# A tokeniser whose gate weights are loaded once for TensorE, and an attention start with a PSUM bank for each piece

## The chip, the cores and the metric

The kernel runs on one core of one Trainium2 chip. The metric is the device time of one execution in microseconds (us). The kernel before took 2230.97 us (median of three runs, 2230.33 to 2231.43). All numbers are fp32 in memory.

## What is computed

Eight images of 256x256 are passed through a three-level Haar wavelet, gated, and rebuilt; the rows of each image and 77 text rows form 333 tokens of width 256. Four pairs of attention and feed-forward layers follow. The change touches the first two parts only:

```python
a1, det1 = haar(x);  a2, det2 = haar(a1);  a3, det3 = haar(a2)   # det: 3 bands each
gate_a   = sigmoid(flat(a3) @ Wa + ba)                            # 1 number per image
gate_l   = softmax(flat(det_l) @ Wd_l + bd_l)                     # 3 numbers per image and level
h        = inverse_haar(gate_a * a3, gate_l * det_l)              # 8 x 256 x 256
h        = concatenate([h, txt], axis=1)                          # 8 x 333 x 256
h        = h + attention16(layernorm(h))                          # 16 heads of 16
```

The dots of the gates run over 12288 numbers for each of the three outputs at the finest level.

## The kernel before

**Tiling.** `tokenise` (L118) puts 16 image rows of one image on one partition, so 16 partitions hold an image and 128 hold all eight. VectorE does the analysis (L240 to L258). The gate weights of each of ten outputs are replicated in SBUF: each image's 16 partitions get their own copy, by 40 DMAs (L161), and VectorE multiplies and sums them with ten `tensor_tensor_reduce` (L270, L277). One small matmul with a matrix of ones per image (L232) sums over 16 partitions; VectorE and ScalarE form sigmoid and softmax (L282 to L307). VectorE then does the synthesis (L320 to L328), level 1 in two halves. SyncE writes each half of the image to a scratch tensor in DRAM (L165, 16 DMAs, one for each half and batch element) and reads it back with 111 tokens on the partitions (L169 for token tiles 0 and 1 of an element; ScalarE issues the 34 image rows of tile 2 at L224). VectorE computes mean and variance per element (L107 to L112), GpSimd a Newton-like refinement of the inverse root in seven operations (L194 to L206). A block ends with a barrier of all engines, and `attention16` is the next block.

**First attention.** Batch elements are pipelined. For an element, `norm` makes `xn`, TensorE transposes it (pieces "x"), makes q and k (pieces "qk", four of them), v (pieces "v"), then scores. All pieces share one PSUM bank `psM`: piece n+1 waits until piece n has been copied out (`piece_out`). q and k are split in a high and a low part; SyncE writes both to DRAM (L482, L483) and reads them back in stacks (L492, eight DMAs of 16 partitions for each of the four pieces). `scores` wait for the stacks (`stack_in`). For batch element 0 the pieces stand in `START`, ahead of the loop; TensorE's first piece waits for all constants (`consts` 3), among them memsets of GpSimd. Then `scores` runs nine steps ahead of the exponentials, and VectorE's `largest` (L567) takes the maxima of each score tile; for the other elements the pieces are put between steps by the table `AT`.

What orders the work here is the program order on each engine and the two hardware DMA queues, one of SyncE and one of ScalarE.

Of the kernel before, what the change touches and what calls it, by code (L numbers as in the profile page):

```python
# [24 lines left out]
B = 8  # L25
# [9 lines left out]
E = 8  # L35

# [14 lines left out]
class Shared:  # L51
# [15 lines left out]
    def early(self, ctx):  # L67

        sb = lambda name, shape: ctx.enter_context(self.nc.sbuf_tensor(name, shape, F32))
        self.cols = sb("cols", [128, len(CNAMES), KT])  # L70
        self.rows = sb("rows", [TT, len(RNAMES), D])
        self.w_last = sb("w_last", [128, 3, KT, D])
        self.weights_in = ctx.enter_context(self.nc.semaphore("weights_in"))
        self.late_weights_in = ctx.enter_context(self.nc.semaphore("late_weights_in"))
# [43 lines left out]
def tokenise(nc, sh, ins, h0):  # L118
    RB = 16
    n1, n2, n3 = 8 * 128, 4 * 64, 2 * 32  # L120
    with ExitStack() as ctx:
        sb = lambda name, shape, dt=F32: ctx.enter_context(nc.sbuf_tensor(name, shape, dt))
        sem = lambda name: ctx.enter_context(nc.semaphore(name))
# [6 lines left out]
        a3 = sb("a3", [128, 2, 32])  # L130
        det = [sb("det1", [128, 3, n1]), sb("det2", [128, 3, n2]), sb("det3", [128, 3, n3])]
        wd = [sb("wd1", [128, 3, 3 * n1]), sb("wd2", [128, 3, 3 * n2]), sb("wd3", [128, 3, 3 * n3])]
        wa = sb("wa", [128, n3])
        gb = sb("gb", [128, 10])
        gs = sb("gs", [128, 10])
        group = sb("group", [128, 128])
        dots = sb("dots", [128, 10])
# [3 lines left out]
        ps = ctx.enter_context(nc.psum_tensor("ps_gate", [128, 512], F32))  # L141
        var2 = sb("var2", [TT, NT])
        wa_in, txt_in, h_done = (sem(n) for n in ("wa_in", "txt_in", "h_done"))
        img_in = [sem(f"img_in{i}") for i in range(2)]
        h0_out, h_in = ([sem(f"{n}{b}") for b in range(B)] for n in ("h0_out", "h_in"))
        wd_in = [[sem(f"wd_in{lv}{j}") for j in range(3 if lv == 0 else 1)] for lv in range(3)]
        dots_done, summed, z_ready, exp_done, image_ready, group_ready = (
            sem(n) for n in ("dots_done", "summed", "z_ready", "exp_done", "image_ready", "group_ready"))
        const_ready = sem("const_ready")
        block = ctx.enter_context(nc.Block())  # L150

        @block.sync
        def _(sync):
            rows = ins["x"].rearrange("(p r) c -> p r c", r=RB)
            for half in range(2):
                sync.dma_start(img[:, 8 * half:8 * half + 8, :], rows[:, 8 * half:8 * half + 8, :]).then_inc(img_in[half], 16)
            for lv in (2, 1, 0):
                for j, arrived in enumerate(wd_in[lv]):
                    part = slice(j, j + 1) if lv == 0 else slice(0, 3)
                    for b in range(B):  # L160
                        sync.dma_start(wd[lv][16 * b:16 * b + 16, part, :], ins[f"wd{lv}"][:, part, :]).then_inc(arrived, 16)  # L161
            for half in range(2):
                sync.wait_ge(image_ready, half + 1)
                for b in range(B):
                    sync.dma_start(h0[b, 0:IMG, :].rearrange("(p r) c -> p r c", r=RB)[:, 8 * half:8 * half + 8, :],  # L165
                                   out[16 * b:16 * b + 16, 8 * half:8 * half + 8, :]).then_inc(h0_out[b], 16)
            for b in range(B):
                sync.wait_ge(h0_out[b], 32)
                sync.dma_start(sh.h[:, NT * b:NT * b + 2, :],  # L169
                               h0[b, 0:2 * TT, :].rearrange("(t p) c -> p t c", p=TT)).then_inc(h_in[b], 16)  # L170
            sync.wait_ge(sh.weights_in, 48)

        @block.gpsimd
        def _(pool):
            nc.gpsimd.memset(sh.ident[:, :], 0.0)
            nc.gpsimd.memset(group[:, :], 1.0)
            nc.gpsimd.memset(sh.eps[:, :], EPS)
            nc.gpsimd.memset(sh.mhalf[:, :], -0.5)
            pool.drain()
            nc.gpsimd.affine_select(out=sh.ident[:, :], in_=sh.ident[:, :], compare_op=ALU.not_equal, fill=1.0,  # L180
                                    base=0, pattern=[[-1, 128]], channel_multiplier=1)
            g3 = group[:, :].rearrange("p (g r) -> p g r", r=16)
            nc.gpsimd.affine_select(out=g3, in_=g3, compare_op=ALU.is_ge, fill=0.0,
                                    base=0, pattern=[[-16, 8], [0, 16]], channel_multiplier=1)
            pool.drain()
            nc.gpsimd.affine_select(out=g3, in_=g3, compare_op=ALU.is_ge, fill=0.0,
                                    base=15, pattern=[[16, 8], [0, 16]],
                                    channel_multiplier=-1).then_inc(group_ready, 1)
            g = nc.gpsimd
            eps, mh = sh.eps[0:TT, 0:NT], sh.mhalf[0:TT, 0:NT]  # L190
            for b in range(B):
                pool.wait_ge(h_done, b + 1)
                var, r = sh.mv[:, NT * b:NT * b + NT, 1], sh.rs[:, NT * b:NT * b + NT]
                g.tensor_tensor(var2[:, :], var, eps, ALU.add)  # L194
                pool.drain()
                g.tensor_tensor(r, var2[:, :], mh, ALU.pow)
                pool.drain()
                g.tensor_tensor(var2[:, :], r, r, ALU.mult)
                pool.drain()
                g.tensor_tensor(var2[:, :], var2[:, :], var, ALU.mult)  # L200
                pool.drain()
                g.tensor_tensor(var2[:, :], var2[:, :], eps, ALU.add)
                pool.drain()
                g.tensor_tensor(var2[:, :], var2[:, :], mh, ALU.pow)
                pool.drain()
                g.tensor_tensor(r, r, var2[:, :], ALU.mult)  # L206
                pool.drain()

        @block.scalar
        def _(act):  # L210
            act.dma_start(wa[:, :], ins["wa"]).then_inc(wa_in, 16)
            act.dma_start(gb[:, :], ins["gb"].partition_broadcast(128)).then_inc(wa_in, 16)
            act.dma_start(sh.cols[:, :, :], ins["cols"]).then_inc(sh.weights_in, 16)
            act.dma_start(sh.h[IMG - 2 * TT:TT, 2:NTILES:NT, :], ins["txt"].rearrange("b q c -> q b c")).then_inc(txt_in, 16)
            for arrived in wd_in[0]:
                act.wait_ge(arrived, 16 * B)
            act.dma_start(sh.w[:, 0:3, :, :], ins["w"][:, 0:3, :, :]).then_inc(sh.weights_in, 16)
            act.dma_start(sh.rows[:, :, :], ins["rows"].partition_broadcast(TT)).then_inc(sh.weights_in, 16)
            act.wait_ge(z_ready, 1)
            nc.scalar.activation(ez[:, 0:1], z[:, 0:1], ACT.Exp, scale=-1.0)  # L220
            nc.scalar.activation(ez[:, 1:10], z[:, 1:10], ACT.Exp).then_inc(exp_done, 1)
            for b in range(B):
                act.wait_ge(h0_out[b], 32)
                act.dma_start(sh.h[0:IMG - 2 * TT, NT * b + 2, :], h0[b, 2 * TT:IMG, :]).then_inc(h_in[b], 16)  # L224
            act.dma_start(sh.w[:, 3:, :, :], ins["w"][:, 3:NW, :, :]).then_inc(sh.late_weights_in, 16)
            act.dma_start(sh.w_last[:, :, :, :], ins["w"][:, NW:, :, :]).then_inc(sh.late_weights_in, 16)

        @block.tensor
        def _(pe):
            pe.wait_ge(group_ready, 1)  # L230
            pe.wait_ge(dots_done, 1)
            nc.tensor.matmul(ps[:, 0:10], group[:, :], dots[:, :], start=True, stop=True).then_inc(summed, 1)  # L232

        @block.vector
        def _(dve):
# [7 lines left out]
            def analysis(src, rows, cols, approx, details):  # L243
# [3 lines left out]
                if src is img:  # L247
                    for half in range(2):
                        dve.wait_ge(img_in[half], 16)
                        columns(img, 8 * half, 8 * half + 8, cols)  # L250
                else:
                    columns(src, 0, rows, cols)
                dve.drain()
                dt = details[:, :, :].rearrange("p j (r c) -> p j r c", c=cols // 2)
                v.tensor_tensor(approx, s_[:, 0:rows:2, :], s_[:, 1:rows:2, :], ALU.add)
                v.tensor_tensor(dt[:, 0], s_[:, 0:rows:2, :], s_[:, 1:rows:2, :], ALU.subtract)
                v.tensor_tensor(dt[:, 1], d_[:, 0:rows:2, :], d_[:, 1:rows:2, :], ALU.add)
                v.tensor_tensor(dt[:, 2], d_[:, 0:rows:2, :], d_[:, 1:rows:2, :], ALU.subtract)  # L258
                dve.drain()

            analysis(img, 16, 256, a1[:, :, :], det[0])
            analysis(a1, 8, 128, a2[:, :, :], det[1])
            analysis(a2, 4, 64, a3[:, :, :], det[2])
# [4 lines left out]
            dve.wait_ge(wa_in, 32)  # L268
# [2819 lines left out]
```

## Time and profile before

| | us |
|---|---|
| median of three runs | 2230.97 |
| the profiled execution | 2230.21 |
| its span, first to last instruction | 2228.4 |
| last dot of the gates | 56.25 |
| image rebuilt | 77.31 |
| attention's first instruction | 135.00 |
| its first scores on TensorE | 161.99 |
| share of TensorE / VectorE / ScalarE / GpSimd busy | 80% / 51% / 33% / 24% |

The first column of a row of the timeline is the start in us from the span's start, the second the time from the start of the first to the end of the last of the instructions merged in it; then engine, line, operation, output<-input and count. In brackets stands the idle time of the engine before it and what ended it. SPq and ACTq are the DMA issues of SyncE and ScalarE; the DMA itself ends later. The profiled execution's time is 1.8 us more than its span, which is what lies before the first and after the last instruction.

### The profile page before, as it was taken

The numbers are of one execution on the slowest core, as the hardware profiler recorded it, in microseconds if no ns is written. First come the engines' busy times: TensorE is split into PE (matmuls) and PEld (weight loads), VectorE is DVE, ScalarE is ACT, GpSimd is POOL, SyncE is SP. The second block draws the span as 40 slices with busy tenths as digits, with TensorE's granted clock in tenths as the row PEclk, the third lists the DMA queues.
The fourth block names the chain that finished last, engine by engine and source line by source line (L and its number), as shares of the span: only waits on it lengthen the run. The fifth ranks groups of instructions, "written<-read, shape, count | busy, mean of one in ns | idle before, by whom it ended". The sixth has DMA issues, their size and how long they took to land. (4 is left out here: it accounts for less than half of the span.)

```text
span 2228.4 us, 32244 instructions
## 1 busy us (share of the span) xinstructions
PE 1791.9 (80%) x9490; PEld 1172.1 (53%) x9490; DVE 1134.6 (51%) x3610; ACT 746.4 (33%) x1845; POOL 538.0 (24%) x761
## 2 busy tenths in 40 slices
PE   0039999998897989977884999748998998983998
PEld 0014444443564667755552776515665666652676
DVE  4437767675325576655542344336665666640111
ACT  0004444444231125421221111027665666631211
POOL 0040101000301012221212333204444454531122
PEclk9999999999998889989996999959999999995999
DMA  8435445451940000043111121031000010002341
GB/s 170 141 75 90 95 81 103 80 88 35 360 169 0 1 1 1 1 202 120 30 33 34 58 63 59 23 111 67 15 26 21 26 26 20 20 19 60 135 145 62
DMA packets 82997, 159.48 MB, mean 72 GB/s; under 512 B 24374, under 2 KB 66245, under 8 KB 78127
## 3 DMA queue, kind: packets, MB, share of 16 engines
q1 hardware_dynamic: 61081, 131.96, 21.5%
q0 software_dynamic: 19872, 19.73, 3.4%
q10 hardware_dynamic: 1893, 5.99, 0.9%
q8 instruction: 67, 1.10, 0.2%
q14 instruction: 84, 0.69, 0.1%
HBM read 96.20 MB, written 64.62 MB: 72 GB/s over the span
## 5 line engine op out<-in xcount | busy, mean ns | idle before, releaser
L2371 POOL TENSOR_SCALAR l_P<-l_P,l_ri 111x111 f32<-111x111 f32 (+1 forms) x256 | 177.5, 710 | 215.2 <-DVE l_ri L2540 214.9
L2630 ACT ACTIVATE l_P<-l_S,l_nm 111x111 f32<-111x111 f32 (+2 forms) x384 | 179.3, 471 | 37.6 <-DVE l_nm L2533 37.3
L666 ACT ACTIVATE PT<-psT 111x666 f32<-111x666 f32 x192 | 139.3, 726 | 155.8 <-PE psT L747 155.4
L567 DVE TENSOR_REDUCE mx<-psS 111x2 f32<-111x666 f32 x192 | 159.7, 848 | 25.9 <-PE psS L732 25.9
L758 PE MATMUL psO<-PT,vS 111*32 111x333 f32 x768 | 147.6, 463 | 0.1
L2750 PE MATMUL l_psP<-ident,l_P 111*111 111x111 f32 x768 | 104.7, 274 | 31.9 <-DVE l_PT L2549 26.7
L2750 PEld LDWEIGHTS l_psP<-ident,l_P 111*111 111x111 f32 x768 | 91.6, 182 | 62.9 <-issue 34.8
L2533 DVE CUSTOM_DVE_ANT_0 l_S<-l_psA,l_am 111x111 f32<-111x111 f32 (+1 forms) x256 | 79.1, 331 | 76.3 <-PE l_psA L2736 59.4
L2147 PE MATMUL t_psH<-expert_w,t_xT 128*128 x224 | 103.1, 605 | 1.5 <-DVE t_xT L2081 1.2
L534 POOL TENSOR_TENSOR low<-raw,high 128x333 f32<-128x333 f32 x32 | 28.6, 893 | 307.8 <-DVE high L579 307.8
L2170 PE MATMUL t_psY<-expert_w,t_hT 128*128 x448 | 101.6, 380 | 0.9 <-DVE t_yb L2097 0.7
L2025 ACT ACTIVATE t_hg<-t_psH 128x512 f32<-128x512 f32 x56 | 33.4, 597 | 186.9 <-PE t_psH L2147 186.9
L2721 PE MATMUL l_psM<-l_wo,l_oT 128*111 128x256 f32 x384 | 89.4, 387 | 8.0 <-ACT l_oT L2644 7.0
L2762 PE MATMUL l_psO<-l_PT,l_vS 111*64 111x333 f32 (+2 forms) x768 | 90.5, 372 | 0.6 <-ACT l_oT L2644 0.6
L2639 ACT ACTIVATE l_P<-l_P,l_ri 111x333 f32<-111x333 f32 x128 | 66.2, 565 | 69.1 <-DVE l_ri L2540 69.0
L2170 PEld LDWEIGHTS t_psY<-expert_w,t_hT 128*128 128x128 f32 x448 | 82.9, 190 | 11.7 <-issue 1.5
L2972 PE MATMUL c_psY<-c_w,c_hT 128*111 128x256 f32 x384 | 84.2, 379 | 0.6 <-DVE c_yb L2919 0.6
L700 PE MATMUL psM<-ident,xn 111*128 111x111 f32 x48 | 10.6, 343 | 91.4 <-POOL vS L527 81.9
L2955 PE MATMUL c_psH<-c_xT,c_w 128*128 128x333 f32 x256 | 75.7, 454 | 8.6 <-DVE c_xT L2905 6.5
L744 PE MATMUL psT<-qs,ks 64*111 64x334 f32 x384 | 79.6, 410 | 3.2 <-DVE mT L595 0.7
L107 DVE BATCH_NORM_STATS2 moments<-h 111x6 f32<-111x256 f32 (+1 forms) x168 | 60.5, 416 | 40.9 <-DMA h<-h_scratch 36.4
L2721 PEld LDWEIGHTS l_psM<-l_wo,l_oT 128*111 128x111 f32 x384 | 66.8, 179 | 24.4 <-issue 5.1
(394 smaller groups left out, 3752.5 us busy)
## 6 DMA issues: line engine op xcount, KB each, us to landing
xs_scratch<-zeros SPq DMA_DIRECT2D x30, 896.0 KB, 23.8
expert_w<-in_moe_dram SPq DMA_DIRECT2D x8, 2048.0 KB, 24.9
c_w<-in_moe_dram SPq DMA_DIRECT2D x16, 1024.0 KB, 7.4
qs<-halves_scratch SPq DMA_DIRECT2D x128, 83.5 KB
ks<-halves_scratch SPq DMA_DIRECT2D x128, 83.5 KB, 4.0
halves_scratch<-high SPq DMA_DIRECT2D x32, 167.0 KB, 4.2
halves_scratch<-low SPq DMA_DIRECT2D x32, 167.0 KB, 4.7
c_xb<-xs_scratch SPq DMA_DIRECT2D x8, 667.3 KB
```

The source lines that it names most:

```text
L567: v.tensor_reduce(mx[J % 2][:, t, c:c + 65:64], psS[s % 2][0:TT, :, 0:T], AX.X, ALU.max, negate=True).then_inc(max_done, 1)
L666: s_.activation(PT[jp % 2][:, :, a, :], psT[0:TT, :, 0:T], ACT.Exp).then_inc(exp_done, 1)
L744: mm(psT[0:TT, half, 0:TE], ks[p][ph, jp, qt(a)], qs[p][ph, jp, :], start=True, stop=False)
L758: r = mm(psO[at:at + 32, 0:T], vS[p][:, a, h, :], PT[jp % 2][:, half, a, :], start=a == 0, stop=a == NT - 1)
L2147: r = mm(psH[s % 2][q][:, :], xT[s % 2][:, k, :], experts.w[:, e, 1024 * k + 512 * q:1024 * k + 512 * q + 512], start=k == 0, stop=k == KT ...
L2170: r = mm(psY[:, 0:D], hT[s % 2][:, c, :], experts.w[:, e, at:at + D], start=c == 0, stop=c == 7)
L2371: r = g.tensor_scalar(Pt, Pt, ri[:, c % 2, 2 * t + half:2 * t + half + 1], None, ALU.mult)
L2630: s_.activation(P[c % 4][:, half, at(t):at(t + 1)], Sm[:, half, at(t):at(t + 1)], ACT.Exp, bias=nm[:, c % 2, i:i + 1], scale=-1.0, accum_o ...
L2721: r = mm(psM[0:TT, 0:D], oT[p][:, c, qt(j)], wo[:, c, :], start=c == 0, stop=c == NC - 1)
L2750: r = nc.tensor.transpose(psP[0:TT, half, qt(i)], P[c % 4][:, half, at(t) + TT * a:at(t) + TT * a + TT], sh.ident[0:TT, 0:TT])
L2762: r = mm(psO[64 * half:64 * half + 64, TT * a:T], vS[p][:, a, DH3 * kv:DH3 * kv + DH3], PT[c % 2][:, half, a, TT * a:T], start=a == 0, sto ...
L2972: r = mm(psY[t % 2][0:TT, 0:D], hT[p][:, f, qt(t)], stream.w[p][:, at:at + D], start=f == 0, stop=f == NF - 1)
```

## The change

**Weights.** One tensor `wd` of 128 x 1568 numbers, laid out so that the partition is a column of the image data within a chunk of 128; each weight is there once. **Dots.** TensorE transposes the 32 chunks of 128x128 of the details and `a3` (eight groups of four, six PSUM banks), ScalarE copies each group to SBUF, TensorE multiplies with the weights of the chunk, for all 16 row groups at once; VectorE picks each partition's own row group with `own`, and the old small matmul sums over the 16 partitions. **Synthesis.** For levels 2 and 1 ScalarE scales two of the detail bands and GpSimd adds and subtracts them; VectorE keeps the rest. **Image in and out.** Four loads of a quarter; the image goes out in three DMAs instead of 16; element 0 is read back first, the seven others by two DMAs of SyncE (one for token tile 0, one for tile 1, each 111 partitions x 7 rows of 1 KB) and one of ScalarE (34 partitions x 7). Their arrival is waited for in the attention (`h_rest`). **Statistics.** Only element 0's are in `tokenise`; those of element 1 come after VectorE's `START` pieces, those of elements 2 to 7 in the first body, one at every fourth step. The inverse root is one power on GpSimd. **Late weights** are issued right after the image, not after the read-back. **Attention.** Each of the first eight pieces has a PSUM bank of its own; most of GpSimd's memsets come after its first four `lower`; ScalarE issues the first stacks of k, after its `START` pieces.

```diff
-            for b in range(B):
-                sync.wait_ge(h0_out[b], 32)
-                sync.dma_start(sh.h[:, NT * b:NT * b + 2, :],
-                               h0[b, 0:2 * TT, :].rearrange("(t p) c -> p t c", p=TT)).then_inc(h_in[b], 16)
+            sync.wait_ge(image_ready, 1)
+            sync.dma_start(h0_rows[:, 0:8, :], out[:, 0:8, :]).then_inc(h0_half, 16)
+            sync.wait_ge(image_ready, 2)
+            sync.dma_start(h0_rows[0:16, 8:16, :], out[0:16, 8:16, :]).then_inc(h0_first, 16)
+            sync.dma_start(h0_rows[16:128, 8:16, :], out[16:128, 8:16, :]).then_inc(h0_rest, 16)
...
+            sync.dma_start(sh.h[:, 0:2, :], h0[0:2 * TT, :].rearrange("(t p) c -> p t c", p=TT)).then_inc(h_first, 16)
+            sync.wait_ge(h0_rest, 16)
+            later = h0[IMG:B * IMG, :].rearrange("(b q) c -> q b c", q=IMG)
+            for t in range(2):
+                sync.dma_start(sh.h[:, NT + t:NTILES:NT, :], later[t * TT:(t + 1) * TT]).then_inc(sh.h_rest, 16)
...
+            for g in range(NG):
+                act.wait_ge(turn_done, g + 1)
+                nc.scalar.activation(turned[:, g, :], psG[g % NTURN][:, :], ACT.Copy).then_inc(turn_out, 1)
...
+            def dot(g):
+                pe.wait_ge(turn_out, g + 1)
+                for i in range(4):
+                    at, n, w, first, last = weights(4 * g + i)
+                    r = nc.tensor.matmul(psD[:, at:at + n], turned[:, g, 128 * i:128 * i + 128], w, start=first,
+                                         stop=last, skip_group_check=True)
...
+                for i in range(4):
+                    r = nc.tensor.transpose(psG[g % NTURN][:, 128 * i:128 * i + 128], chunk(4 * g + i), sh.ident[:, :])
+                r.then_inc(turn_done, 1)
+                if g > 0:
+                    dot(g - 1)
...
+def entry_stats(nc, vector, sh, b):
+    batch_stats(nc, vector, sh, b)
+    return nc.vector.tensor_scalar(sh.rs[:, NT * b:NT * b + NT], sh.batch_mv[:, :, 1], 1.0 + EPS, EPS * EPS, ALU.mult,
+                                   ALU.add)
...
+        first_bank = [psM, psO, psS[0][:, 0, :], psS[0][:, 1, :], psS[1][:, 0, :], psS[1][:, 1, :], psT[:, 0, :],
+                      psT[:, 1, :]]
...
+            dve.wait_ge(consts, 1)
+            dve.wait_ge(sh.h_rest, 48)
+            entry_stats(nc, dve, sh, 1).then_inc(entered, 1)
             for s in range(AHEAD):
                 largest(0, s)
...
+                    if first and s % 4 == 2:
+                        entry_stats(nc, dve, sh, 2 + s // 4).then_inc(entered, 1)
...
             for n, (kind, j) in enumerate(START):
                 piece(kind, j, 0, 0, n)
+            first_keys(1)
+            first_keys(3)
```

## Rows read from the trace of the kernel before

**Rows 1.** The page, TensorE's busy tenths in 40 slices of 55.7 us.

```profile
PE   0039999998897989977884999748998998983998
```

**Rows 2.** Timeline, VectorE's analysis and dots.

```profile
10.34 1.23 DVE L240 TENSOR_TENSOR haar_s<-img 128x1024 f32<-128x1024 f32 x1 [1.65 <-DMA img<-in_x_dram]
...
21.35 0.22 DVE L258 TENSOR_TENSOR det<-haar_d 128x64 f32<-128x64 f32 x1
...
32.96 3.36 DVE L277 CUSTOM_DVE_ANT_0 img_out<-det,wd 128x3072 f32<-128x3072 f32 x1 [6.23 <-DMA wd<-in_wd_dram]
...
56.17 0.08 DVE L277 DVE_READ_ACCUMULATOR2_ANT dots<- 128x1 f32 x1
```

**Rows 3.** Timeline, gates and synthesis on VectorE.

```profile
57.01 0.17 DVE L282 TENSOR_TENSOR z<-ps_gate,gs 128x10 f32<-128x10 f32 x1 [0.76 <-PE ps_gate L232]
...
60.53 0.28 DVE L320 SCALAR_TENSOR_TENSOR haar_s<-det,ez,a 128x64 f32<-128x64 f32 x1
...
65.92 0.75 DVE L320 SCALAR_TENSOR_TENSOR haar_s<-det,ez,a 128x512 f32<-128x512 f32 x1
...
76.09 1.22 DVE L328 TENSOR_TENSOR img_out<-haar_s,haar_d 128x1024 f32<-128x1024 f32 x1
```

**Rows 4.** Timeline, the way of the tokens through DRAM and their statistics.

```profile
71.69 9.81 SPq L165 DMA_DIRECT2D h_scratch<-img_out  x16
...
81.54 35.62 SPq L169 DMA_DIRECT2D h<-h_scratch  x8
85.56 0.37 ACTq L225 DMA_DIRECT2D w<-in_w_dram  x1
...
93.75 1.08 DVE L107 BATCH_NORM_STATS2 moments<-h 111x6 f32<-111x256 f32 x3 [16.45 <-DMA h<-h_scratch]
...
125.77 1.08 DVE L107 BATCH_NORM_STATS2 moments<-h 111x6 f32<-111x256 f32 x3 [1.35 <-DMA h<-h_scratch]
```

**Rows 5.** Stage view: last columns are granted clock, DMA share, GB/s.

```profile
115.00:123.00 8.00, 0.00 (x0) 0.00 (x0) 3.48 (x16) 0.00 (x0) 5.72 (x15) 1.00 0.20 71
```

**Rows 6.** Timeline of SyncE alone, one issue of a token load.

```profile
87.00 16.97 SPq L169 DMA_DIRECT2D h<-h_scratch  x1
```

**Rows 7.** Timeline, the start of the first attention up to the first scores.

```profile
134.40 0.19 POOL L206 TENSOR_TENSOR rs<-rs,var 111x3 f32<-111x3 f32 x1
...
135.00 2.07 DVE L559 TENSOR_SCALAR xn<-h,mv,rs 111x256 f32<-111x256 f32 x3 [7.20 <-PEq L121]
...
138.89 0.81 PE L700 MATMUL psM<-ident,xn 111*128 111x111 f32 x3 [81.92 <-POOL vS L527]
...
142.03 2.59 PE L704 MATMUL psM<-xT,w 128*128 128x333 f32 x4 [0.72 <-ACT xT L651]
...
146.80 0.36 SPq L482 DMA_DIRECT2D halves_scratch<-high  x1
...
154.80 3.71 SPq L492 DMA_DIRECT2D ks<-halves_scratch  x8
...
161.99 0.56 PE L732 MATMUL psS<-ks,qs 64*111 64x334 f32 x4 [1.37 <-DMA ks<-halves_scratch]
```

**Rows 8.** Timeline, four kinds of work of which the change adds more.

```profile
56.40 0.57 PE L232 MATMUL ps_gate<-dots,group 128*128 128x10 f32 x2 [56.40 <-DVE dots L277]
...
145.82 0.89 POOL L534 TENSOR_TENSOR low<-raw,high 128x333 f32<-128x333 f32 x1 [6.99 <-DVE high L579]
...
755.79 0.82 PE L1102 MATMUL s_psT<-ident,s_y 128*111 128x128 f32 x6
...
1021.67 1.25 PE L1880 MATMUL m_psV<-m_wr,m_rT 128*111 128x8 f32 x12
```

**Rows 9.** The page, costliest groups: a copy of 128x512 out of PSUM.

```profile
L2025 ACT ACTIVATE t_hg<-t_psH 128x512 f32<-128x512 f32 x56 | 33.4, 597 | 186.9 <-PE t_psH L2147 186.9
```

**Rows 10.** Timeline, TensorE's piece of rows 7 once more, in the loop.

```profile
177.41 1.39 PE L704 MATMUL psM<-xT,w 128*128 128x333 f32 x4
```

**Rows 11.** Stage view of most of the first body: PE, PEld, DVE, ACT, POOL busy.

```profile
176.00:213.50 37.50, 37.35 (x242) 18.03 (x242) 24.28 (x52) 17.70 (x27) 3.57 (x4) 0.99 0.59 111
```

More of the change, by code:

```diff
@@ new lines, in tokenise, with det_of, chunk @@
+        img_in = [sem(f"img_in{i}") for i in range(4)]
+        h0_half, h0_rest = sem("h0_half"), sem("h0_rest")
+        block = ctx.enter_context(nc.Block())
+        def det_of(g):
+            c = 4 * g
+            return 1 + c // 8 if c < G1 else 4 if c + 4 <= G1 + G2 else 5
+        def chunk(c):
+            if c < G1:
+                return det1[:, :, :].rearrange("p j n -> p (j n)")[:, 128 * c:128 * c + 128]
+            if c < G1 + G2:
+                c -= G1
+                return det2[:, :, :].rearrange("p j n -> p (j n)")[:, 128 * c:128 * c + 128]
+            c -= G1 + G2
+            return low3[:, :, :].rearrange("p j n -> p (j n)")[:, 128 * c:128 * c + 128]
@@ L189, in _ @@
[L189 to L207, printed above, removed]
+            g.affine_select(out=g3, in_=g3, compare_op=ALU.is_ge, fill=0.0,
+                            base=15, pattern=[[16, 8], [0, 16]],
+                            channel_multiplier=-1).then_inc(group_ready, 1)
@@ new lines, in _ @@
+            for n in range(3):
+                cols, r0, r1 = ((64, 0, 4), (128, 0, 4), (128, 4, 8))[n]
+                lv = 1 if n == 0 else 0
+                part = slice(r0 * cols, r1 * cols)
+                hi = (hi2 if lv else hi1)[:, 2 * r0:2 * r1, :]
+                a, b = (e[lv][:, part].rearrange("p (r c) -> p r c", c=cols) for e in (e1, e2))
+                pool.wait_ge(e_ready, n + 1)
+                g.tensor_tensor(hi[:, 0:8:2, :], a, b, ALU.add)
+                g.tensor_tensor(hi[:, 1:8:2, :], a, b, ALU.subtract).then_inc(hi_ready, 1)
@@ L221, in _ @@
             nc.scalar.activation(ez[:, 1:10], z[:, 1:10], ACT.Exp).then_inc(exp_done, 1)
[L222 to L226, printed above, removed]
+            act.wait_ge(ez_ready, 1)
@@ new lines, in _ @@
+            for lv, part in ((1, slice(0, n2)), (0, slice(0, n1 // 2)), (0, slice(n1 // 2, n1))):
+                w = 4 if lv else 7
+                nc.scalar.activation(e1[lv][:, part], det[lv][:, 1, part], ACT.Copy, scale=ez[:, w + 1:w + 2])
+                nc.scalar.activation(e2[lv][:, part], det[lv][:, 2, part], ACT.Copy,
+                                     scale=ez[:, w + 2:w + 3]).then_inc(e_ready, 1)
+            act.wait_ge(h0_half, 16)
+            act.wait_ge(h0_first, 16)
+            act.dma_start(sh.h[0:IMG - 2 * TT, 2, :], h0[2 * TT:IMG, :]).then_inc(h_first, 16)
@@ L230, in _ @@
+            dot(NG - 1).then_inc(dots_done, 1)
             pe.wait_ge(group_ready, 1)
-            pe.wait_ge(dots_done, 1)
-            nc.tensor.matmul(ps[:, 0:10], group[:, :], dots[:, :], start=True, stop=True).then_inc(summed, 1)
+            pe.wait_ge(dots_ready, 1)
+            nc.tensor.matmul(psZ[:, 0:10], group[:, :], dots[:, :], start=True, stop=True).then_inc(summed, 1)
         @block.vector
@@ L247, in analysis @@
                 if src is img:
-                    for half in range(2):
-                        dve.wait_ge(img_in[half], 16)
-                        columns(img, 8 * half, 8 * half + 8, cols)
+                    for i in range(4):
+                        dve.wait_ge(img_in[i], 16)
+                        columns(img, 4 * i, 4 * i + 4, cols)
                 else:
@@ L326, in synthesis @@
+                if n is None:
+                    v.tensor_scalar(dt[1], dt[1], w(1), None, ALU.mult)
+                    dve.drain()
+                    v.scalar_tensor_tensor(hi[:, 0:rows:2, :], dt[2], w(2), dt[1], ALU.mult, ALU.add)
+                    v.scalar_tensor_tensor(hi[:, 1:rows:2, :], dt[2], nw(2), dt[1], ALU.mult, ALU.add)
+                else:
+                    dve.wait_ge(hi_ready, n + 1)
                 dve.drain()
                 v.tensor_tensor(dst[:, :, 0:2 * cols:2], lo, hi, ALU.add)
-                r = v.tensor_tensor(dst[:, :, 1:2 * cols:2], lo, hi, ALU.subtract)
@@ L435, in attention16, with bank @@
         own = lambda kind, j: kind == "ot" and j < 3 or kind == "most" and j > 0
+        def bank(n):
+            return first_bank[n] if isinstance(n, int) and n < len(first_bank) else psM
         def begin(b):
@@ L502, in batch @@
                     stack(b, p, n)
-                    stack(b, p, n + 1)
+                    if some(b):
+                        stack(b, p, n + 1)
             sync.wait_ge(zero_cols, 1)
@@ L547, in body @@
                         lower(b + 1, n)
+                if first:
+                    for n in range(2, B):
+                        entry(n)
                 if not first:
@@ L693, in piece @@
             def piece(kind, j, b, p, n):
-                if some(n):
+                if not isinstance(n, int) or n >= N0:
+                    pe.wait_ge(piece_out, n)
+                elif n == 2:
+                    pe.wait_ge(piece_out, 2)
+                elif n == N0 - 1:
                     pe.wait_ge(piece_out, n)
```

255 lines of the change are left out of this document (147 added, 108 removed).

## The prediction

> **What bounds the kernel now.** I read the page's slices first: TensorE does nothing in the first two slices and is at nine tenths or more in most that follow [rows 1]. So the end is set by TensorE's work, and by when that work begins: whatever is taken from the time before the first scores at 161.99 [rows 7] is taken from the end, as long as what follows is the same work. Then the timeline of the first 162 us. It falls into four stretches. To 56.25 VectorE waits for replicated weights: the analysis is over at 21.6, but the dots of the last level wait three times for a DMA, and the last is read at 56.17 [rows 2]. To 77.31 gates and synthesis, a chain on VectorE alone [rows 3]. To 134.6 the tokens' way through DRAM, the statistics, and GpSimd's seven operations per element [rows 4, 7]. To 161.99 pieces, halves and stacks of element 0 [rows 7]. What lies behind is 2228.4 - 162.0 = 2066.4 us of span.
>
> **Dots.** The last image rows are in at 10.34 [rows 2]. With 0.8 MB of weights beside them instead of behind I take 10.5; the columns of the last quarter cost two operations of half of 1.23 and the first band one of 1.23, so TensorE can begin at 13.2. It has eight groups of four transposes and four narrow matmuls, which are two instructions each. From below, at the full clock: 4 x 0.82/6 + 8 x 1.25/12 = 1.4 us a group [rows 8], 11 us in all, but the last group's data come at about 20.7, so the dots can't end before 24. From above, at half clock: 4 x 0.81/3 [rows 7] + 8 x 0.57/2 [rows 8] = 3.4 us a group, 27 us; with 3 us until ScalarE, which first issues six DMAs and loads its table, gives back the first copy, they end at 44. ScalarE's copies, 0.6 us [rows 9] for each group, hide beside either. Of the clock: the same piece takes 2.59 at 142 [rows 7] and 1.39 at 177 [rows 10], so TensorE began the attention at half its 2.4 GHz, and with gaps between pieces stayed there. Here it is fed without gaps, so I expect it to begin at half and rise on the way: about 1.9 us a group after the first copy at 16.5, the end at 31. That is 25 us earlier than 56.2.
>
> **Gates and synthesis.** Two more VectorE operations and a hop add about 1.0. From the dots to the first synthesis operation lie 60.53 - 56.25 = 4.3 [rows 3], less one drained operation, 0.2: 5.1 in all. Synthesis took 77.31 - 60.53 = 16.8 [rows 3]. Levels 2 and 1 lose the three operations that make the high part: two halves of 2 x 0.75 + 0.48 (the third is a tensor_scalar), and 1.4 for level 2, 5.4 in all. They go to ScalarE and GpSimd. GpSimd's 0.89 for 333 columns [rows 8] makes 1.37 for 512 and 0.68 for 256: four at 1.37 and two at 0.68 are 6.9 us, which beside VectorE's 10 us of level 3, 2 and the first half just keeps up (its parts would be ready 0.5 to 1.5 us before VectorE asks). So 11.4 us if the two engines don't hinder one another, and up to 6.9 more if each of GpSimd's six operations holds VectorE up for its whole length, which would give back all that was moved away. The trace of before has no stretch in which VectorE adds out of SBUF beside such an operation of GpSimd, so I take half, 3.5: 14.9 us. The image is rebuilt at 31 + 5.1 + 14.9 = 51, 26.3 earlier. The Trainium skill, in "SBUF — State Buffer", section "Who interferes with whom", says that a VectorE instruction with two SBUF inputs and a GpSimd instruction that reads SBUF contend, and the later of the two fully blocks. By that rule the upper end holds, and the time would be 3.4 us above my sum. No row here decides it.
>
> **The way through DRAM.** I call the rebuilt image's time R. The first half is written from R - 3.7, the second from R, in three DMAs. Before, 2 MB went out over 9.8 us of issues [rows 4], some 210 GB/s; so the 1 MB of the second half has landed at R + 6. Element 0's tokens land behind it at R + 9.5; statistics 1.9, of which 1.08 are the three of one row [rows 4], one power on GpSimd 0.9, barrier 0.4: the attention could begin at R + 13. Removed for good are the other seven elements' loads and statistics from the path (93.8 to 125.8) and GpSimd's tail to 134.6 [rows 4, 7].
>
> But here is what is late next. While only token loads run, the DMA share is 0.20 at 71 GB/s [rows 5]: three of sixteen engines carry them (111 is three times 37), 43 ns for a row of 1 KB on each. The seven other elements are 2 x 777 rows on SyncE's queue and 238 on ScalarE's, again 111 and 34 partitions. Two engines get 259 + 259 + 119 = 637 rows, 27.4 us; from R + 8.5 they end at R + 36. Nothing shortens that, and it has two effects. SyncE's issue of a token load is held up while the queue is full: one took 16.97 us [rows 6], and the last ended at 117.2, 8.5 us before its data at 125.7. So SyncE ends its last issue at R + 28, and arrives at the barrier then: all engines wait for it. And the halves of q and k, issued on the same queue, stand behind those rows. From the attention's start A: norm 2.1 [rows 7], two transposes without waiting between them to A + 4.5 (before: A + 7.0, since GpSimd's memsets held TensorE to 138.89 [rows 7]), the first q written at A + 9.5 (before 146.80 - 135.0 = 11.8), the second piece at A + 12, ScalarE's stack of k from A + 16.7 to 20.3 instead of SyncE's to 158.5 - 135.0 = 23.5, scores 3.4 after it: A + 23.7 instead of A + 27.0. So 3.3 us is what the banks, the memsets and ScalarE's issues bring; between 0 (ScalarE's issues are slowed as two engines share one set of DMA engines) and 6.
>
> With A = R + 28.4 = 79.4, scores begin at 103.1, which is 58.9 us earlier. h_rest, asked by VectorE before its first `largest`, is in by R + 37 and hides. Were SyncE not held up, the queue's rows would still put the halves at R + 36 and scores at R + 44.5, 7.5 earlier.
>
> **Statistics in the first body.** Six times 1.85 us, 11.1 us more on VectorE in a stretch of 42 in which it is busy 24.28/37.5 = 65%, or 27 us [rows 11]: 38 of 42. `largest` has two steps of slack, so I take 2 us, between 0 and 8. GpSimd has time. Late weights earlier cost nothing: they are done before R, and no longer delay element 0's load, as they did (issued at 85.56, load landed at 93.7 [rows 4]).
>
> **Sum.** 58.9 - 2 = 57 us. 2230.21 (the profiled run, 1.8 over its span and 0.8 under the median) - 57 = 2173; by the median, 2174.
>
> **Rivals.**
> (1) The read-back doesn't hold the start: rows are spread over more engines, or are all taken into the queue at once and the halves pass them. Then A = R + 13 and scores at R + 37 = 88: 74 - 2 saved, 2159. For it: stacks and halves use all engines, and only before's loads of 222 rows show the limit. Against: the share of 0.20 and the issue of 16.97 [rows 5, 6] with the same 111 partitions. 15%.
> (2) TensorE stays at half clock through the tokeniser and VectorE is the bound in the first body: dots at 41, 10 later, and 6 more in the body: 41 saved, 2190. For it: half clock until 158 in the attention at 80% busy; against: no gaps here. 15%.
> (3) Slower: the reordered read-back. Its rows follow one another by batch element, 256 KB apart in DRAM, where before they were neighbours of 1 KB. If such a row costs four times 43 ns, the 637 rows take 110 us instead of 27: scores at 186, and the kernel 26 us slower, 2257. It decides from 43 x (27.4 + 57)/27.4 = 132 ns a row. For it: no load of before has that stride; against: at 24 GB/s an engine, each row is limited by the engine, not the memory. 3%. The Trainium skill, in "DMA: Bandwidth & Descriptors", section "Latency and other measured facts", says that large power-of-two pitches in HBM cut copies from about 210 to 103 GB/s (at 4 MB; 207 still at 512 KB); at 256 KB it would thus change nothing, and no run here shows it.
> The forecast itself has 65%, with 2163 to 2185 as its own range; 2% for anything else.
>
> **How the numbers follow.** About 5 us can be told from no change here (0.2%). The range of 8 in 10 is the forecast's own, plus most of (1) and half of (2): 2153 to 2188. Faster 0.96, same 0.01, slower 0.03.
>
> **What would show it.** Right: last narrow matmul near 31; image at 51; an issue of a token load of over 15 us on SyncE, and attention's first instruction right after it, near 79, with all other engines idle since about 64; a DMA share near 0.2 for 25 us; scores near 103; the rest of the span, from there to the end, 2068. Wrong: the attention beginning at R + 13, a stretch of the loads at over 100 GB/s, or a first body over 50 us long. A span behind the first scores that is off 2066 by over 8 us would say that something I hold to be the same is not.

## The result: 2171.05 us, and the profile after

| us | before | after | forecast |
|---|---|---|---|
| median | 2231.2 (2230.33 to 2232.52, 4 runs) | 2171.05 (2169.34 to 2175.37, 4 runs) | 2174 (2153 to 2188) |
| ratio, 95% interval | | 0.9733 (0.9716 to 0.975) | |
| span of the profiled execution | 2228.4 | 2173.6 | |
| last dot | 56.25 | 35.59 | 31 |
| image rebuilt | 77.31 | 57.04 | 51 |
| attention's first instruction | 135.00 | 78.34 | 79.4 |
| first scores | 161.99 | 107.47 | 103.1 |
| from there to the end | 2066.4 | 2066.1 | 2068 |

The profiled execution is the slowest of the four (2175.37). Its gain of 54.8 us in span is there before the first scores (54.5); the medians differ by 60.

The timeline after, in the order of the chain. The dots and the gates, which answer to [rows 2, 3]:

```profile
15.12 1.94 PE L289 MATMUL ps_turn<-ident,det 128*128 128x128 f32 x8 [15.12 <-DVE det L319]
...
22.26 1.78 PE L278 MATMUL ps_dots<-wd,det_turned 128*128 128x48 f32 x8
...
35.63 0.33 DVE L338 TENSOR_TENSOR prod<-ps_dots,own_row 128x160 f32<-128x160 f32 x1 [13.10 <-PE ps_dots L278]
...
40.03 0.28 DVE L382 SCALAR_TENSOR_TENSOR haar_s<-low_band,ez 128x64 f32<-128x64 f32 x1
40.36 0.71 ACT L262 ACTIVATE e<-det,ez 128x512 f32<-128x512 f32 x1
40.50 0.85 DVE L383 SCALAR_TENSOR_TENSOR haar_s<-low_band,z 128x64 f32<-128x64 f32 x1 [0.18 <-issue]
40.54 0.73 POOL L236 TENSOR_TENSOR hi<-e 128x256 f32<-128x256 f32 x1 [37.89 <-ACT e L263]
...
43.18 1.30 DVE L388 SCALAR_TENSOR_TENSOR haar_d<-low_band,z 128x64 f32<-128x64 f32 x1
...
44.35 1.26 POOL L236 TENSOR_TENSOR hi<-e 128x512 f32<-128x512 f32 x1
44.55 1.22 DVE L392 TENSOR_TENSOR a<-haar_s,haar_d 128x128 f32<-128x128 f32 x1
...
55.82 1.22 DVE L393 TENSOR_TENSOR img_out<-haar_s,hi 128x1024 f32<-128x1024 f32 x1
```

TensorE paces the dots: it is busy for 20.34 of the 20.48 us from 15.12, at 2.45 us a group. And VectorE's small operations at 40 to 47 take about as long as GpSimd's beside them: an operation of 128x64 takes 0.28 at 40.03 and 1.30 at 43.18.

Then the way through DRAM and the attention's start, which answer to [rows 4, 6, 7]:

```profile
60.17 0.31 SPq L205 DMA_DIRECT2D h<-h_scratch  x1
...
63.52 14.29 SPq L209 DMA_DIRECT2D h<-h_scratch  x2
...
67.38 1.08 DVE L109 BATCH_NORM_STATS2 moments<-h 111x6 f32<-111x256 f32 x3 [10.33 <-issue]
...
69.23 0.89 POOL L239 TENSOR_TENSOR rs<-rs,mhalf 111x3 f32<-111x3 f32 x1 [22.35 <-DVE rs L410]
...
78.34 1.75 DVE L654 TENSOR_SCALAR xn<-h,mv,rs 111x256 f32<-111x256 f32 x3 [9.19 <-PEq L126]
...
86.95 2.02 SPq L566 DMA_DIRECT2D halves_scratch<-high  x1
...
94.33 1.08 DVE L109 BATCH_NORM_STATS2 moments<-h 111x6 f32<-111x256 f32 x3 [1.56 <-DMA h<-h_scratch]
95.24 3.61 SPq L576 DMA_DIRECT2D qs<-halves_scratch  x8
...
107.47 0.90 PE L848 MATMUL psS<-ks,qs 64*111 64x334 f32 x4 [15.16 <-issue]
```

At 70.12 all compute is done, but SyncE issues token loads until 77.8, and the attention begins half a microsecond after it. The rows of elements 1 to 7 land at 94.3; only then have q's first halves landed, although SyncE issued them at 87 to 89.5. The stage view says how they are moved (last columns: granted clock, DMA share, GB/s), with [rows 5]:

```profile
64.00:78.00 14.00, 0.00 (x0) 0.00 (x0) 1.63 (x8) 0.00 (x0) 0.89 (x1) 1.00 0.20 70
```

### The profile page after: what moved, and what is told of

The parts are those of the page before. It is cut to its first block and busy times, and to the rows that moved or that the text cites. A ratio compares the mean times of both kernels' runs of the same rounds, so it can differ in the third digit from the quotient of the medians.

```text
span 2173.6 us, 32276 instructions
## 1 busy us (share of the span) xinstructions
PE 1809.4 (83%) x9586; PEld 1192.9 (55%) x9586; DVE 1121.5 (52%) x3596; ACT 753.5 (35%) x1859; POOL 529.3 (24%) x719
## 5 line engine op out<-in xcount | busy, mean ns | idle before, releaser
L2261 PE MATMUL t_psH<-expert_w,t_xT 128*128 x224 | 103.1, 605 | 1.6 <-DVE t_xT L2195 1.2
L848 PE MATMUL psS<-ks,qs 64*111 64x334 f32 x384 | 64.6, 332 | 17.8 <-issue 15.2
L2876 PEld LDWEIGHTS l_psO<-l_PT,l_vS 111*64 111x64 f32 x768 | 52.3, 144 | 48.6 <-issue 16.0
```

The source lines that it names most:

```text
L2261: r = mm(psH[s % 2][q][:, :], xT[s % 2][:, k, :], experts.w[:, e, 1024 * k + 512 * q:1024 * k + 512 * q + 512], start=k == 0, stop=k == KT ...
L2876: r = mm(psO[64 * half:64 * half + 64, TT * a:T], vS[p][:, a, DH3 * kv:DH3 * kv + DH3], PT[c % 2][:, half, a, TT * a:T], start=a == 0, sto ...
```

## The experiments

A kernel's total scatters: the four to six runs of a changed kernel lie 6 to 20 us apart (those of the kernel before, 9 to 11 at a time beside them, 7 to 18), where its stages up to the first scores repeat far better (eight kernels with the same tokeniser have the image rebuilt at 56.6 to 57.1, and two profiled runs of the kernel after have their first scores at 107.47 and 106.06). So the small edits are judged by their stages, and the totals by their medians. The kernel after was run again with the last experiments (e11_after): 2175.48 (2168.15 to 2184.04); its nine runs have the median 2172.5.

The traces show where the scatter lies. From the first scores to the end the 14 profiled executions take 2059.9 to 2076.2 us, and TensorE's busy time in that stretch, for the same 9454 instructions, is 1770.1 to 1788.3; what is left beside it is 288 to 293 in all of them. So nearly all of the spread is TensorE taking longer for the same work. One body of the first attention, the work of one batch element, shows it: the fourth, in the kernel after and in its second profiled run, e11_after (columns: PE, PEld, DVE, ACT, POOL busy, granted clock, DMA share, GB/s).

```profile
262.60:309.18 46.58, 45.32 (x288) 21.61 (x288) 33.77 (x81) 20.94 (x32) 4.57 (x6) 0.96 0.44 89
```

```profile
259.83:309.13 49.30, 48.05 (x288) 22.89 (x288) 33.88 (x82) 21.18 (x32) 4.58 (x6) 0.90 0.47 84
```

The same kernel and the same 288 instructions, 2.7 us more at a granted clock of 0.90 instead of 0.96. What makes the clock differ between two runs is not shown.

**e1_spread: the rows of elements 1 to 7 over more engines.**

```diff
             for t in range(2):
-                sync.dma_start(sh.h[:, NT + t:NTILES:NT, :], later[t * TT:(t + 1) * TT]).then_inc(sh.h_rest, 16)
+                for a, zz in ((0, 96), (96, TT)):
+                    sync.dma_start(sh.h[a:zz, NT + t:NTILES:NT, :], later[t * TT + a:t * TT + zz]).then_inc(sh.h_rest, 16)
```

(ScalarE's 34 partitions are cut at 32 in the same way.)

> The read-back of elements 1 to 7 is cut at 96 and 32 partitions, so that its rows are spread over more DMA engines; nothing else changes. Theory (three engines set the start of the attention, through SyncE's held issue, and the halves stand behind the rows): the two issues take under 4 us instead of 14.3, the attention begins at about 70.5 instead of 78.3, the rows are in by 80 instead of 94.3, and the first scores come at about 95.5 instead of 107.5: 12 us less, about 2159 us. Rival A (the memory, not the engines, limits the rows): DMA rate stays near 70 GB/s, the attention begins where it did, 2171. Rival B (the rows held only SyncE, while the 12 us from the first stack to the scores are what the stacks' own data take and are not shortened): attention 8 us earlier and the scores 8 us earlier, 2163.

Measured 2163.31 (2154.04 to 2169.98), ratio to before 0.9688 (0.9659 to 0.9717). The timeline and the stage view of this kernel:

```profile
63.40 1.91 SPq L210 DMA_DIRECT2D h<-h_scratch  x4
...
70.90 1.75 DVE L657 TENSOR_SCALAR xn<-h,mv,rs 111x256 f32<-111x256 f32 x3 [1.30 <-PEq L126]
...
79.51 0.35 SPq L569 DMA_DIRECT2D halves_scratch<-high  x1
...
82.52 3.73 SPq L579 DMA_DIRECT2D qs<-halves_scratch  x8
...
93.75 0.89 PE L851 MATMUL psS<-ks,qs 64*111 64x334 f32 x4 [8.96 <-issue]
```

```profile
68.00:70.00 2.00, 0.00 (x0) 0.00 (x0) 1.45 (x8) 0.00 (x0) 0.32 (x1) 1.00 1.15 201
```

The DMA rate goes from 70 to about 200 GB/s, the four issues take 1.9 us, the attention starts 7.4 us earlier and the scores 13.7. Of these, 7.4 are the barrier, and most of the rest is the halves: 3.0 us from the first issue to the first stack instead of 8.3. Both effects that the prediction named are shown. Rivals A and B fall. The medians differ by 8 to 9 us (2171.05, or 2172.5 over nine runs, to 2163.31); what is missing of the 13.7 is within the scatter. Only this cut was tried, so the runs show that the 111 partitions held the rate down, but not which partition counts do.

**e2_dve_synth: the synthesis on VectorE alone** (ScalarE's six scalings and GpSimd's six additions go; three of VectorE's come back in each of three parts).

```diff
-            synthesis(a2[:, :, :], det[1], 4, 0, 4, 64, a1, 0)
+            synthesis(a2[:, :, :], det[1], 4, 0, 4, 64, a1)
...
-                synthesis(a1[:, :, :], det[0], 7, 4 * half, 4 * half + 4, 128, out, 1 + half).then_inc(image_ready, 1)
+                synthesis(a1[:, :, :], det[0], 7, 4 * half, 4 * half + 4, 128, out).then_inc(image_ready, 1)
```

> The synthesis goes back to VectorE alone; ScalarE and GpSimd take no part. Theory (VectorE and GpSimd took turns, so that what was moved away came back as waiting): VectorE's level 3 operations return from 0.7 to 1.3 us each to under 0.3, the synthesis takes 16.8 us instead of 17.0, and the time stays at 2171 within 1 us. Rival (they ran beside one another and something else, such as ScalarE's scaling, made VectorE wait): 16.8 us against what would be 11.4 with the parts in time, and level 3 operations stay slow; the kernel then is 2 to 5 us slower, 2174.

Measured 2171.26 (2167.81 to 2179.03). Its timeline:

```profile
39.98 0.28 DVE L367 SCALAR_TENSOR_TENSOR haar_s<-low_band,ez 128x64 f32<-128x64 f32 x1
...
41.17 0.28 DVE L373 SCALAR_TENSOR_TENSOR haar_d<-low_band,z 128x64 f32<-128x64 f32 x1
41.52 0.29 DVE L377 TENSOR_TENSOR a<-haar_s,haar_d 128x128 f32<-128x128 f32 x1
...
55.80 1.22 DVE L378 TENSOR_TENSOR img_out<-haar_s,haar_d 128x1024 f32<-128x1024 f32 x1
```

The image is rebuilt at 57.02, with GpSimd's help at 57.04. What GpSimd took over came back as waiting. ScalarE was not the cause: in e12_all_cold below it scales at the same time, VectorE's 128x64 operations stay under 0.3, and the synthesis takes 15.1 us.

**e3_warm: TensorE busy ahead of the first detail.**

```diff
             pe.wait_ge(ident_ready, 1)
+            for i in range(90):
+                nc.tensor.transpose(psZ[:, 128 * (i % 4):128 * (i % 4) + 128], sh.ident[:, :], sh.ident[:, :])
             pe.wait_ge(wd_in, 16)
```

> TensorE runs 90 transposes of the identity into an unused PSUM bank before the first detail is there; nothing else changes. Theory (the dots took until 35.6 because TensorE ran them at half of 2.4 GHz, 2.45 us a group): it reaches full level before 15 us, a group takes 1.3 us, the dots end near 26, and all that follows comes 9.5 us earlier: 2161.5. Rival A (ScalarE's copies or semaphore hops pace the groups): the end of the dots moves by under 3 us, 2168. Rival B (the earlier image is given back behind the rows, which take as long as before): the dots are 9.5 earlier but the first scores less than 5.

```profile
1.92 11.41 PE L284 MATMUL ps_gate<-ident 128*128 128x128 f32 x90 [1.92 <-POOL ident L220]
15.19 1.06 PE L291 MATMUL ps_turn<-ident,det 128*128 128x128 f32 x8 [1.86 <-DVE det L321]
...
25.00 1.96 PE L278 MATMUL ps_dots<-wd,det_turned 128*128 128x48 f32 x16
```

Eight transposes take 1.06 instead of 1.94 and sixteen narrow matmuls 1.96 instead of 3.52, so in the kernel after TensorE had run all the dots at half its 2.4 GHz. (The stage view prints 1.00 for that stretch, too; ahead of the first recorded change of clock the durations decide.) The dots end at 26.96 and the first scores come at 98.12, 9.3 us earlier: rivals A and B fall. But the total, 2171.46 (2164.3 to 2183.5), does not show it; e8_all and e12_all_cold below take that up.

**e4_old_start: one PSUM bank and SyncE's issues of k again.** The two edits are those of e5 and e6 below, here without the spread.

> The start of the first attention goes back to one PSUM bank for all pieces and to SyncE's issue of the first k stacks; GpSimd's memsets stay where the change put them. Theory (both are hidden behind the rows of elements 1 to 7, which are in at 94.3 only): the q halves are written 1 to 2 us later but land at the same time, and the first scores come at 107.5 to 109, so the time is 2171 to 2173. Rival (they gave the 3.3 us of the prediction): scores at 111, 2174.5.

Measured 2173.37 (2165.78 to 2174.91); first scores at 106.17, 1.3 us before those of the kernel after, whose attention began 1.0 later. Behind the rows the two edits are worth nothing. GpSimd's memsets stayed where the change put them.

**e5_spread_one_bank** and **e6_spread_sync_keys: each half of the old start, with the rows out of the way.**

```diff
 def bank(n):
-            return first_bank[n] if isinstance(n, int) and n < len(first_bank) else psM
+            return psM
```

```diff
                     stack(b, p, n)
-                    if some(b):
-                        stack(b, p, n + 1)
+                    stack(b, p, n + 1)
...
-            first_keys(1)
-            first_keys(3)
```

(In e5_spread_one_bank TensorE also waits before each piece until the one before is copied out, as it did before the change.)

> The spread read-back of e1_spread, and one PSUM bank for all first pieces again, each waiting for the one before to be copied out. With the rows out of the way nothing covers the pieces. Theory (the banks are worth what the gaps between pieces cost): k's halves are written about 2.5 us later, the first scores come at 96 instead of 93.75, and the time is 2 to 3 us above e1_spread. Rival (the 12 us from the first stack to the scores absorb it): scores stay at 93.75.

> The spread read-back, and SyncE issues the first k stacks again, after those of q. Theory (sixteen stack loads of 16 partitions each take about 11.3 us of DMA time whoever issues them, as before the change and in e4_old_start): first scores at 93.5 to 94.5 as in e1_spread. Rival (issue is the bound, 3.7 us for eight): scores at 96 to 97.5.

Counted from the attention's start, the first scores come after 22.9 us in e1_spread (70.90 to 93.75), 25.2 in e5 (70.66 to 95.85) and 23.0 in e6 (71.58 to 94.59). The totals are 2164.38 (2160.31 to 2169.49) and 2155.46 (2154.5 to 2162.7), too scattered to tell them from e1_spread. The banks are worth 2.3 us once nothing covers them, ScalarE's issues 0.2. Why the issues are worth nothing stands in e6's timeline and the stage view of the kernel after:

```profile
83.11 3.60 SPq L579 DMA_DIRECT2D qs<-halves_scratch  x8
...
94.59 0.90 PE L848 MATMUL psS<-ks,qs 64*111 64x334 f32 x4 [10.01 <-issue]
```

```profile
98.00:100.00 2.00, 0.00 (x0) 0.00 (x0) 0.00 (x0) 0.00 (x0) 0.00 (x0) 0.50 1.13 120
```

Sixteen stacks take 11.5 us here from the first issue to the scores, 11.0 to 11.3 in the other two kernels with one issuer (before, e4_old_start), and 10.9 to 12.2 with two. From 98 to 106 in the kernel after the DMA share is 1.07 to 1.13, so all engines are busy, at 120 to 250 GB/s, and who issues doesn't matter.

**e7_stats_twice** and **e9_stats_early: the statistics in the first body, doubled, and moved ahead of the first scores.**

```diff
                     if first and s % 4 == 2:
+                        entry_stats(nc, dve, sh, 2 + s // 4)
+                        dve.drain()
                         entry_stats(nc, dve, sh, 2 + s // 4).then_inc(entered, 1)
```

```diff
-            entry_stats(nc, dve, sh, 1).then_inc(entered, 1)
+            for e in range(1, 7 + 1):
+                entry_stats(nc, dve, sh, e).then_inc(entered, 1)
...
-                    if first and s % 4 == 2:
-                        entry_stats(nc, dve, sh, 2 + s // 4).then_inc(entered, 1)
```

> The kernel after the change with the statistics of elements 2 to 7 computed twice in the first body, 6 x 1.85 = 11 us more on VectorE. Theory (VectorE is near its limit there, so the first body grew from 46.8 to 51.2 us by them): the body grows by 8 to 12 us more, to 60. Rival (VectorE has slack, and the 4.4 us came from the half clock at its start): under 4 us more.

> The kernel after the change with the statistics of all seven later elements ahead of the first scores, in the 11 us in which VectorE waits there, and none in the first body. Theory (e7: they stand in full on the path of the first body, where VectorE is at its limit): the first body takes 47 to 48 us instead of 51.2, the first scores stay at 107, and the time is 3 us less. Rival (first body and clock, not VectorE): body unchanged at 50 to 51.

The first body, from one `norm` to the next, with its stage view (PE, PEld, DVE, ACT, POOL busy, granted clock, DMA share, GB/s): before, after, in e7 and in e9.

```profile
170.74:217.52 46.78, 46.41 (x291) 22.37 (x292) 31.28 (x68) 22.01 (x33) 3.57 (x4) 0.94 0.53 96
```

```profile
116.43:167.61 51.18, 48.04 (x291) 22.85 (x291) 39.49 (x117) 22.02 (x33) 8.64 (x10) 0.91 0.45 83
```

```profile
115.67:177.72 62.05, 52.89 (x291) 24.82 (x291) 49.21 (x164) 22.02 (x33) 8.65 (x10) 0.85 0.35 67
```

```profile
115.74:161.40 45.66, 45.40 (x291) 21.94 (x291) 31.21 (x68) 21.80 (x33) 8.52 (x10) 0.96 0.52 95
```

VectorE is busy 31.3 of 46.8 us before, 39.5 of 51.2 after and 49.2 of 62.0 in e7. The second statistics (six times 1.85 us from start to end, 9.7 us of them busy) make the body 10.9 longer: TensorE's idle time in it grows from 3.1 to 9.2 us, and its busy time for the same 291 instructions from 48.0 to 52.9, at a granted clock of 0.85 instead of 0.91. In e9 it lasts 45.7, with the first scores at 106.77: the seven statistics fit into the wait for the stacks, and the body is 5.5 shorter.

The totals of e7 and e9, 2173.43 and 2171.18 (2167.54 to 2174.65), move by less than the scatter; against e11_after's 2175.48, run beside it, e9 is 4.3 less. That e7's total does not show its 10.9 us has a reason in the trace. Its third to sixth bodies take 181.6 us (227.60 to 409.19) at a granted clock of 1.00 throughout, where they take 188.0 in the kernel after and 193.9 in e11_after, with bodies at 0.90 to 0.96 among them. From the start of the first body to the end of the sixth e7 needs 293.5 us, the kernel after 286.1 and e11_after 290.4: of the 10.9 us 3 to 7 are left. This is one trace, and how the clock comes to differ is not shown.

**e8_all, e10_best and e12_all_cold: the edits together.** e8 has e1's spread, for element 0 too, e3's transposes, and a synthesis in which ScalarE scales and VectorE adds. e10 is e8 with the statistics of elements 1 to 4 early, of which those of element 1 already were. e12 is e8 without the 90 transposes.

```diff
                 else:
-                    dve.wait_ge(hi_ready, n + 1)
+                    lv = 0 if n else 1
+                    e = [x[lv][:, r0 * cols:r1 * cols].rearrange("p (r c) -> p r c", c=cols) for x in (e1, e2)]
+                    dve.wait_ge(e_ready, n + 1)
+                    v.tensor_tensor(hi[:, 0:rows:2, :], e[0], e[1], ALU.add)
+                    v.tensor_tensor(hi[:, 1:rows:2, :], e[0], e[1], ALU.subtract)
```

> All that the runs so far point to: read-back of all elements spread over more engines, TensorE busy with 90 transposes before the first detail, and in the synthesis ScalarE scales but VectorE adds, GpSimd takes no part. Expected from the stages: dots end at 27, synthesis 15.3 us, image at 46.7, attention at 59 since element 0's rows land 2 us sooner, first scores at 81.5 instead of 107.5: 26 us less, 2145. If TensorE's clock over the rest of the kernel takes back what the warm-up gains, as e3_warm's total of 2171 allows, 2155. If element 0's rows are not sooner, 2147.

> e8_all with the statistics of elements 1 to 4 ahead of the first scores, three left in the first body. Expected: first scores at 79.5 as in e8_all, first body 48.5 to 49.5 instead of 51.0, time 2145 (2 us under e8_all, which the spread of the runs may hide).

> The kernel after the change, unchanged, on the same chip and in the same rounds as e9_stats_early and e10_best, so that these are compared with it and not only with the kernel before. Both theories: 2168 to 2174.

> e8_all without the 90 transposes ahead of the first detail. First scores at 88 instead of 79.4. Theory (behind the first scores the kernel takes the same, and e3_warm's missing gain in total was the spread of the runs): 2155, 8 to 9 us above e8_all. Rival (TensorE's earlier work costs clock later, so that what it gains is given back; e3_warm 2171.5 although its scores were 9.3 us earlier, e10_best 2157.9): 2148 to 2150, with the time behind the first scores 6 us shorter than in e8_all's and e10_best's profiled runs (2076 and 2072).

| | image rebuilt | first scores | median (lowest to highest) | ratio to before, 95% |
|---|---|---|---|---|
| e8_all | 46.2 | 79.39 | 2147.11 (2137.87 to 2157.18) | 0.9611 (0.9589 to 0.9633) |
| e10_best | 46.2 | 79.92 | 2157.90 (2153.38 to 2160.47) | 0.967 (0.9653 to 0.9688) |
| e12_all_cold | 55.2 | 88.12 | 2155.26 (2151.83 to 2158.65) | 0.9651 (0.9624 to 0.9679) |
| e11_after | 56.6 | 106.06 | 2175.48 (2168.15 to 2184.04) | 0.9736 (0.9714 to 0.9759) |

All three beat both kernels, with every run below every run of the kernel after. Whether the transposes pay in total stays open: they bring the first scores 8.7 us forward in e8 against e12, and its median is 8.2 lower as the theory had it, while in the profiled executions e12's time behind the first scores is 12.2 us shorter than e8's, as the rival had it; and e10, which has them too, is 2.6 above e12, and e3 no faster than the kernel after. Behind the first scores the three profiled kernels with them took 2070.6, 2076.0 and 2072.2 us; ten of the other eleven, the kernel before among them, took 2059.9 to 2072.3, and e11_after 2076.2. An estimate from the medians (less 1.8 us and the first scores of the profiled execution) gives 2065.9 to 2076.2 for the three and 2059.1 to 2068.5 for the others: it leans to a part being given back, and doesn't settle it.

e10's total missed its forecast of 2145 by 13 us, and its first body its 48.5 to 49.5. The stage views of that body in e8 and in e10:

```profile
88.35:139.35 51.00, 47.88 (x291) 22.78 (x291) 39.48 (x116) 22.04 (x33) 8.65 (x10) 0.92 0.42 82
```

```profile
88.89:139.53 50.64, 49.10 (x291) 23.31 (x291) 35.72 (x92) 21.95 (x33) 8.52 (x10) 0.88 0.40 82
```

With three of the body's six statistics moved out, VectorE has 3.8 us less to do and TensorE's idle time falls from 3.1 to 1.5. But TensorE's own time for the same 291 instructions is 1.2 longer, at a granted clock of 0.88 instead of 0.92, and takes most of it back.

## Why the prediction was right, step by step

The sum was 57 us and the medians gave 60, the profiled spans 54.8. What carried it was right: the kernel gains what the time before the first scores loses, and SyncE's held issue sets the start of the attention. The terms were less good:

- **Dots**: 31 forecast, 35.6 measured. The failed part is "I expect it to begin at half and rise on the way": TensorE stayed at half level, although it was fed without gaps (2.45 us a group; 1.28 at full clock in e3). My upper bound of 3.4 us a group was far too high, as it took the length of short isolated runs for the pace in a stream: 0.285 for a narrow instruction where it is 0.22 (1.78 for eight).
- **Synthesis**: 14.9 forecast, between 11.4 and 18.3; 17.0 measured, and 17.0 with GpSimd's part taken away (e2). The step "I take half" was the wrong choice: the Trainium skill's rule quoted there, from "SBUF — State Buffer", section "Who interferes with whom", describes what is seen, VectorE's two-input operations at up to 1.34 beside GpSimd's at up to 1.31; 5.6 of the 6.9 us at stake were lost. So the 5.4 us of synthesis that the diff takes from VectorE are worth nothing (16.8 before the change).
- **The read-back**: "three of sixteen engines carry them" and "SyncE's issue of a token load is held up" are both shown by e1. The rows were in 37.3 us after the image, forecast 36. SyncE was free 20.8 us after it, forecast 28: the queue takes more rows than I read out of before's 8.5 us between last issue and last data; here they are 16.5 apart. That error, 7.1, hid the 6.0 us by which the image was late, which is luck. The longest issue took 14.0 us, where over 15 was named as a sign of being right.
- **Start of the attention**: 23.7 us from its first instruction to the scores were forecast, 29.1 measured, since with the earlier start the halves stood behind the rows, the second of my two effects. Uncovered it is 22.9 (e1). That is 4.1 less than before's 27.0, where I credited 3.3 to banks, memsets and issues. The banks make 2.3 of it and ScalarE's issues 0.2 (e5, e6). The sum had the first q 2.3 earlier and the scores 3.3, so 1.0 for the issues; that is wrong, as the stacks are bound by their data. The rest, 1.6, is left for the memsets and whatever else e5 and e6 keep; no run put the memsets back.
- **First body**: 2 forecast, "`largest` has two steps of slack" the reason; 4.4 measured (46.8 to 51.2), and 10.9 more for the second six (e7). The slack covers one delay; six of them, with VectorE busy for 39.5 of 51.2 us, held TensorE up. At 51.2 us the body is over the 50 that the prediction named as a sign of being wrong.
- **The rest**: 2068 forecast, 2066.4 before, 2066.1 after. This agreement is luck in part. It holds although the first body is 4.4 longer, since the five bodies behind it take 234.9 us (167.61 to 402.51) where they took 243.6 before (217.52 to 461.14), two of these at a granted clock of 0.90. In e11_after, the same kernel, they take 239.3 and the rest 2076.2, off by more than the 8 us that the prediction allowed. So "the same work" holds, but not that it takes the same time.

Errors of +4.6 (dots), -0.7 (gates), +2.1 (synthesis), -7.1 (read-back) and +5.4 (start) on the way to the first scores left 4.4: the total was right to 3 us with two terms off by over 5, of opposite signs. Rival (1) fails at 78.34; half of rival (2), the half clock, is what happened; rival (3) is excluded by the profile after itself, where the strided rows come at 70 GB/s at a DMA share of 0.20, as before the change, and are in 37.3 us after the image.

## What to carry to other kernels

Look at the partition count of a load: 111 partitions ran on three engines' worth of DMA, and cutting the loads at 96 (and 32 of 34) took 13.7 us from the first scores; a load that nobody waits for yet still holds its issuer, and with it a barrier, and all that is issued on the same queue. Before work is moved to GpSimd to relieve VectorE, ask whether the two overlap at all; here ScalarE was the engine with something to give. And work "spread over a loop" is not free because the engine has idle time on average: VectorE was busy for 77% of the longer body (39.5 of 51.2) and delayed TensorE by 3 us all the same; in the wait before the loop the same work was free.

## What was not expected of the hardware

- TensorE ran 20 us of gapless transposes and narrow matmuls (20.34 of 20.48 us busy) at half of its clock, but after 11.4 us of 90 transposes of the same shape it was at full level, with a gap of 1.9 us between (e3). In the kernel after it rose in the attention: a matmul of 128x333 every 0.56 us from 82.3 to 87.4, and about every 0.3 behind that. Whether e3's transposes differ by having no matmuls between them or by their data, the identity, was not tried.
- VectorE's operations on 64 columns were stretched from 0.28 to up to 1.30 us beside GpSimd's on 512 columns (the profile after, and e2 without GpSimd).
- Sixteen loads of 16 partitions each, 1.3 MB, take 11 to 12 us whether one or two engines issue them (e6 against e1).
- A changed kernel's runs scatter by 6 to 20 us in total. In the profiled executions it lies behind the first scores, in TensorE's busy time for the same 9454 instructions (1770.1 to 1788.3 us).
- In e7, whose first body is 10.9 us longer, the third to sixth ran at a granted clock of 1.00 and took 6.4 us less than in the kernel after.
